# Type-sorted node tiles of a two-layer graph attention kernel, worked through in dealt order (position = tile number times 11 modulo 64)

## What is computed

```
def typed_linear(x, t, W):            # each node is multiplied by the matrix of its type
    y_all = jnp.einsum('nd,tdo->nto', x, W)
    return jnp.take_along_axis(y_all, t[:, None, None], axis=1)[:, 0]
def gt_layer(...):
    k, q, v = typed_linear(x, ntype, Wk), ... Wq, ... Wv          # n x 8 heads x 16
    kT = einsum('nhd,htdo->nhto', k, Watt)                        # for all 32 edge types
    vT = einsum('nhd,htdo->nhto', v, Wmsg)
    a = einsum('ehd,ehd->eh', kT[src,:,etype], q[dst]) * pri / 4
    att = edge_softmax(a, dst)
    hag = segment_sum(vT[src,:,etype] * att, dst)
    h = silu(typed_linear(hag, ntype, Wa))
    h = h * sigmoid(skip[ntype]) + x * (1 - sigmoid(skip[ntype]))
    return layernorm(h) * g + b
out = layernorm(x + (gt_layer twice)(x) @ ff_w + ff_b)
```

## The kernel before

| positions | 3 | 6 | 10 | 14 | 18 | 22 | 26 | 29 | 33 | 36 | 40 | 44 | 48 | 51 | 55 | 58 | 59 to 63 |
|---|---|---|---|---|---|---|---|---|---|---|---|---|---|---|---|---|---|
| nodes | 21 | 110 | 5 | 5 | 4 | 20 | 5 | 100 | 1 | 122 | 60 | 31 | 37 | 107 | 6 | 112 | 0 |

## Time and profile before

### The profile page before, as it was taken

The page is one execution under the profiler, slowest core; times in us unless marked ns, Lnnn a source line. Parts: engine busy times, 40 slices in busy tenths (PEclk is TensorE's granted clock), DMA queues, the critical chain, the costliest instruction groups (busy, mean ns, idle before and its releaser), DMA issues.

```text
span 3829.7 us, 61710 instructions
## 1 busy us (share of the span) xinstructions
PE 2556.1 (67%) x14673; PEld 1803.2 (47%) x14674; DVE 2719.9 (71%) x6690; ACT 1723.3 (45%) x3944; POOL 2562.5 (67%) x2612
## 2 busy tenths in 40 slices
PE   2777777366666666665577777556766676666587
PEld 1333333255555555554333333245555555555465
DVE  5666666577777777777577777667777777777654
ACT  1666666333333333333467666623343343343332
POOL 3666655677777777772666665577777777776266
PEclk8889888577777767767788889766776766677555
DMA  7999997545545444444799999655554444444222
GB/s 143 360 379 392 409 406 319 155 134 135 136 133 137 135 133 138 135 132 114 223 403 362 386 415 407 215 142 136 139 134 134 134 134 134 139 135 123 74 73 52
DMA packets 302264, 777.66 MB, mean 203 GB/s; under 512 B 69179, under 2 KB 229979, under 8 KB 289423
## 3 DMA queue, kind: packets, MB, share of 16 engines
q0 software_dynamic: 111152, 651.90, 48.6%
q1 hardware_dynamic: 182067, 121.18, 12.4%
q10 hardware_dynamic: 8704, 0.54, 0.2%
HBM read 335.05 MB, written 568.60 MB: 236 GB/s over the span
## 4 chain that ended last, share of the span: by engine, by line
POOL 42%; PE 20%; issue 17%; DMA 9%; ACT 6%; DVE 4%; SPq 1%; DVEq 0%; POOLq 0%; ACTq 0%
POOL region L759 40%; PE bank L1052 10%; DMA relation_table<-region,scatter_node 7%; ACT region L833 4%; PE bank L1073 2%; PE bank L1082 2%; ACT arena L851 1%; PE bank L1170 1%; PE bank L1169 1%; DMA region<-relation_table,key_of 1%; DVE sums L1673 1%; PE bank L1214 1%; PE bank L1168 1%; PE bank L1151 1%; DVE region L1474 1%
## 5 line engine op out<-in xcount | busy, mean ns | idle before, releaser
L759 POOL DMA_INDIRECT region<-relation_table,key_of x1664 | 1638.5, 985 | 519.2 <-issue 502.7
L1214 PE MATMUL bank<-region,arena 128*128 128x136 f32 x3328 | 736.5, 387 | 422.4 <-DVE region L1658 337.7
L1214 PEld LDWEIGHTS bank<-region,arena 128*128 128x128 f32 x3328 | 626.8, 273 | 515.4 <-DVE sums L1673 281.8
L1052 PE MATMUL bank<-sums,arena 128*128 128x512 bf16 x2048 | 666.4, 433 | 289.7 <-ACT region L833 258.9
L1474 DVE COPY region<-bank 128x512 f32<-128x512 f32 x896 | 589.4, 687 | 307.2 <-PE bank L1052 224.5
L950 ACT ACTIVATE arena<-iota_free,minus_dst 128x128 f32<-128x128 f32 x1664 | 528.5, 388 | 544.5 <-PE bank L1214 539.1
L833 ACT COPY region<-bank 128x512 f32<-128x512 f32 x1152 | 618.0, 609 | 136.8 <-PE bank L1052 106.9
L1200 PE MATMUL bank<-region_q,arena 128*128 x4992 | 579.6, 277 | 85.3 <-DVE arena L1644 79.2
L1636 DVE TENSOR_TENSOR region<-bank,region 128x512 f32<-128x512 f32 x416 | 287.3, 691 | 470.5 <-DMA region<-relation_table,key_of 451.0
L1200 PEld LDWEIGHTS bank<-region_q,arena 128*128 128x128 bf16 x4992 | 500.1, 126 | 157.9 <-issue 99.7
L1673 DVE TENSOR_TENSOR sums<-sums,bank 128x136 f32 x1664 | 475.4, 286 | 76.0 <-DVE sums L1673 46.1
(11 more groups left out here) (238 smaller groups left out, 2876.4 us busy)
## 6 DMA issues: line engine op xcount, KB each, us to landing
arena<-edge_places SPq DMA_DIRECT2D x416, 128.0 KB, 3.3
region<-relation_table,key_of POOLq DMA_INDIRECT x1664, 3.2
arena<-segment_flags SPq DMA_DIRECT2D x104, 128.0 KB
sums<-q_rows SPq DMA_DIRECT2D x6, 768.0 KB, 7.3
aggregated_rows<-sums SPq DMA_DIRECT2D x6, 768.0 KB, 5.2
sums<-relation_weight_parts SPq DMA_DIRECT2D x32, 128.0 KB, 8.6
x_sorted<-arena SPq DMA_DIRECT2D x16, 256.0 KB, 12.1
region_q<-x_sorted SPq DMA_DIRECT2D x16, 256.0 KB, 10.1
```

What stands on the lines that cost most here:

```text
L759: pool.indirect_dma_start(out=rows[:, block_.r, q * QUAD + s], out_offset=None, in_=table, in_offset=bass.IndirectOffsetOnAxis(ap=key_of[: ...
L1052: nc.tensor.matmul(bank[TABLE_BANK + k % TABLE_BANKS][:, :], x_spreadT[:, k, :], w_rel[:, k, :], start=True, stop=True).then_inc(table_psu ...
L1214: ins = nc.tensor.matmul(bank[SUM_BANK[q % 2][pair]][:, s * SUMC:(s + 1) * SUMC], onehots[:, at, 2 * pair + s], rows[:, block_.r, slot, RH ...
```

## The change

The tile with number t now stands at position 11 t mod 64 in `gather_node`, `scatter_node`, `tile_type` and `type_of_tile`. DVE works that out in the preparation: `deal` multiplies, rounds to integer, takes the low six bits and turns the result into floats again. It is called twice: for the position of each node's tile (by 11), and for the tile number that stands at each position (by 35, the inverse of 11 modulo 64), from which the tile's type is found. Nothing else is touched.

```
+DEAL, DEAL_BACK = 11, 35
+assert DEAL * DEAL_BACK % SORTED_TILES == 1
...
+            def deal(out_, number, whole, by):
+
+                link(v.tensor_scalar(out_, number, float(by), None, ALU.mult))
+                link(v.tensor_copy(whole, out_))
+                link(v.tensor_single_scalar(whole, whole, SORTED_TILES - 1, ALU.bitwise_and))
+                link(v.tensor_copy(out_, whole))
...
             link(v.tensor_copy(tile_of_node, pos_hi))
+            deal(tile_of_node, tile_of_node, pos_hi, DEAL)
             link(v.tensor_copy(lo_bits_f, lo_bits))
...
-            link(v.tensor_tensor(type_cmp, bc(iota_free[:, 0:SORTED_TILES], 2, NT), bc(first_tile, 1, SORTED_TILES), ALU.is_ge))
+            deal(tile_at, iota_free[:, 0:SORTED_TILES], tile_at_i, DEAL_BACK)
+            link(v.tensor_tensor(type_cmp, bc(tile_at, 2, NT), bc(first_tile, 1, SORTED_TILES), ALU.is_ge))
```

More of the change, by code:

```diff
@@ L325, in gnn_kernel @@
         is_pad = pb[:, 3240:3240 + NTILES]
+        tile_at = pb[:, 7936:7936 + SORTED_TILES]
+        tile_at_i = pb[:, 8000:8000 + SORTED_TILES].bitcast(I32)
         type_f = pb[:, 3472:3472 + SORTED_TILES]
```

## The result

The changed kernel took 3867.1 us (median of four runs, 3864.0 to 3871.9) against 3825.1 us for the kernel before on the same chip: a ratio of 1.0112, 95% interval 1.0094 to 1.0130, so about 42 us or 1.1% slower. Forecast were 3879 us, 55 us slower, within 3848 to 3898. The sign and the main mechanism (gaps in the middle, a bare end) came out as forecast; the loss is 13 us smaller, and the term for the q rows had the wrong sign.

The account below looks back on a forecast made before the run. The landing of each fused stage's last table store was taken to bound the kernel. The terms 20.3 + 3 + 27.6 + 3 + 0.8 + 0.3 = 55.0 us took the median from 3823.7 to 3878.7 us, range 3848 to 3898.

Parts of the forecast that it names:

- The end of the table stores sets everything behind it: The gathers of `attend` run back to back once the last table store lands; moving that landing moves everything after equally.
- The recurrence for the dealt order: Fused stages: store issues and landings computed from four numbers; dealt order +20.3 us in layer 0, +27.6 in layer 1.
- The sign of three last intervals near 10 us: End of each fused stage: the last three tiles wait for buffers, taking 9.7 to 10.6 us each instead of 5.9.
- The gaps: Middle of the fused stage: small tiles leave transfers idle, 25 us between positions 29 and 34, 13 us round 42 and 43.
- The tail's worth: Old stage end: other work behind the last big store, 27.7 and 25.0 us in the two layers, hides all its latency.
- The q rows, +3 in each layer: End of each fused stage: q loads share transfers with the last table stores, adding 0 to 8 us, taken as 3.
- The small terms, 0.8 and 0.3: Eight DVE steps in the preparation add 0.8 us to the chain; the last four scatters in `finish` add 0.3.
- the gap is filled: Rival: transfers stay dense to the stage's end, last store lands 27.7 and 25.0 us earlier: 3772 us, or 3797; 8%.
- The harsher loss: Rival: q loads take all 8 us twice, pace 8.8, clock falls in the small-tile cluster: 3893 us and up; 11%.
- The milder loss: Rival: pace 8.0 in layer 0, q rows taking no share, only the exposed end in layer 1: 3858 us; 16%.

Follow-up runs that it names:

- With late q rows: Dealt order with SP waiting for the last table stores before loading the q rows: 1.0121 of the kernel before, beside 1.0116 for the dealt order as it is.
- the light tiles at the end: Dealt order turned by 32 positions, so the same neighbours but the cluster of small tiles ends the stage: 1.0045 of the kernel before, 17 us slower.
- the end bared alone: Old order turned by five positions, so the empty tiles come first and the stage ends with full ones: 1.0102 of the kernel before, 39 us slower.
- The same order with the steps: Kernel before plus the eight new DVE steps, multipliers 1 and 1 so every tile keeps its position: 1.0002 of the kernel before.
- the run with late q rows: Kernel before, old order, with SP waiting for the last table stores before loading the q rows: 0.9982 of the kernel before, 3815.7 us.
- the other orders: Against the kernel before: old order turned by five 1.0102, dealt order turned by 32 1.0045, small tiles bunched 1.0243, tiles with nodes reversed 1.0014.
- the first four experiments: Against the kernel before: new steps alone 1.0002, old order turned by five 1.0102, dealt order turned by 32 1.0045, small tiles bunched 1.0243.

## Why the prediction was right, and where its sizes were off

- **The end of the table stores sets everything behind it** (from the earlier trace rows): right in every run. The wait of 21.6 us was forecast as a landing 17 to 25 us after the issue.
- **The recurrence for the dealt order**: position 60 at 649.5, last issue at 680.4, last landing at 698.2 in layer 0; measured 652.3, 676.3 and 698.0. In layer 1, counted from its first store, the last landing 608.9 us on; measured 609.3. That the landings are right to half a microsecond is in part luck: the recurrence holds no q rows and the measured landing does. With late q rows the last landing of layer 0 comes 587.9 us after the first store, where the recurrence has 590.5. The last issue came 4 us early: the refill of a buffer by the last tile, charged with 10.5 us, took 6.8 (669.5 to 676.3). That no engine had work for later tiles any more fits this, but no run isolates it. The transfers were the limit there, so it made no difference; with the light tiles at the end it made most of the error. The sign of three last intervals near 10 us failed with it (5.5, 8.3, 10.2), and the first gathers came at 698.8 and 2495.1, not at 705 and 2513.
- **The gaps**: 25 us of idle transfers were forecast between positions 29 and 34; the windows from 370 to 410 have the shares 0.80, 0.51, 0.09 and 0.34, some 23 us. Round positions 42 and 43 it was 13 us; the window from 500 to 520 has a share of 0.42, some 12 us.
- **The tail's worth**: right, and the tail is the larger part. By the medians the end bared alone costs 39 us, empty tiles in the middle alone 17, both 42; by the stages, against the profile before, 30, 16 and 43. Whether the two add up is therefore not settled.
- **The q rows, +3 in each layer**: this term failed, and it is the one that made most of the miss. I weighed what they would take of the big stores and forgot what they already cost at the old end. The last landing of before lay 2.7 and 2.4 us above the recurrence, and the run with late q rows shows them to be behind it: the store lands 2.1 us after its issue instead of 6.5, where the recurrence has 3.8. The term should have been taken between measured ends: about 2 us that the q rows cost in the dealt order, minus 4.4 in the old, so -2.4 a layer instead of +3. That is 11 of the 13 us.
- **The small terms, 0.8 and 0.3**: no larger than the scatter. The same order with the steps is at 1.0002.
- **The rivals**: "the gap is filled" fell. Interleaving did fill the idle windows at the end, and that is where it lost: the transfers were full when `attend` wanted to start. The harsher loss, by a falling clock, didn't come, since the granted clock stayed at 0.88. The milder loss at 3858 was 9 us off, the forecast 12. Its no share for the q rows was nearer to the -2.4 than the +3 was, and its 16.7 us for layer 0 met the 17.3 measured; its 17 us for layer 1 missed the 25.4.

In the old order the engines' regime at the end was covering the backlog of the transfers, so it was worth something where it stood. By the rule of the Trainium skill that spoke for the change (Perfetto Trace Analysis, "Optimization Strategy": interleave regimes in which different engines are the most contended) a gain might be had; the measured 1.0112, and 1.0045 with the same neighbours and the light tiles at the end, show none here. What the Trainium skill says of round robin between queues, a packet at a time (DMA: Bandwidth & Descriptors, "Queues, rings and completion order") agrees with the trace, 161 packets of either queue in 10 us. With packets of 32 KB and 512 bytes such turns are not equal shares: most of the delay fell on the q rows, 18.3 against 8.2 us.

## What to carry to other kernels

Where a stage ends with a wait for its last transfer and is bound by transfers until then, as here, put the pieces that transfer least at its end: their work hides the backlog. Before spreading light pieces evenly, write the buffer ring down as a recurrence of four measured numbers and put both orders through it; here it was within 3 us of the last landings of the old and the dealt order and ranked the other orders rightly, but landed two of them 6 to 7 us too late in layer 0. Give its last steps numbers of their own. Then take every correction to it as a difference of two measured ends, the old one too: a load that starts when the last store does costs something already, and moving it behind the store gave 8 us here for two lines.

## What the runs showed of the hardware

- Two queues of one core took turns packet by packet, whatever the packets' size: 161 packets of 32 KB and 161 of 512 bytes in 10 us. The narrow stream got 0.08 MB through beside 4.23.
- A store to which nothing is written (all its rows out of bounds) is not free: it still sends 144 packets of 4 bytes and lands 2.1 us after its issue with idle transfers, 6.5 us with the q rows beside it.
- Issuing can block: with big stores under way, one of the four q loads held SP for 19.8 us in the changed kernel, where its longest took 2.7 before. It was 15.7 to 22.5 us in all eight stages that ended with big stores and didn't hold the q rows back, and at most 3.1 us in the others.
- The same kernel took 3824 to 3826 us in some comparisons and 4392.7 in one, with the fused stages as usual (566 to 608 us) but 1311 to 1320 us for the gathers of `attend` instead of 1070, and longer stretches behind each `attend` (151 to 153 us instead of 118, and 335 to 342 instead of 303). The results give this comparison the same chip number (14) as the one of the first four experiments above, so that chips differ is not shown by it. In the order before with late q rows POOL waited there as follows; with the usual time it waited 250.7 us for "issue" and 2.4 for PE:

```profile
POOL region L761 <- remote: 152.7, 62, 3.4
POOL region L761 <- PE bank L1216: 116.1, 52, 39.7
```

"remote" is a releaser that the profile can't name. The packets of the gathers' queue took no longer (800 to 1800 us: 29577 packets in 28.8% of the 16 engines' time, against 35712 in 34.8% in the kernel before, both 156 ns each), so it is waiting and not the transfer itself that grew. Whose, stays open. By the same view 743 gathers of 128 rows moved 97.6 MB, so a gathered row is 1 KB, and not 2 as said further up.
